# Two attention layers on one core: the values matmuls ahead of the key and query transposes in one half of the loop

## The chip, the cores and the metric

The kernel runs on one core of one Trainium2 chip. The metric is the device time of one execution in microseconds (us), as the median of several executions. The core has a matmul engine (TensorE, PE in the profile), a vector engine (VectorE, DVE), a scalar engine (ScalarE, ACT), a general engine (GpSimd, POOL) and a queue that issues transfers (SyncE, SP). Each engine runs its own list of instructions in order, and the engines wait for each other on semaphores.

## The reference

The input x is 64 sequences of 128 tokens with 512 features. Two layers are applied to it one after the other, and each adds its result to x. A layer is causal attention with 16 query heads of 64 and a single key and value head, with one extra "null" key and value ahead of the 128:

```python
# layer 0                                  # layer 1
xn = layernorm(x, g_in)                    xn = ln(x, g_norm)
q = heads(xn @ Wq) * scale                 q = l2norm(heads(xn @ Wq)) * q_scale
k, v = split(xn @ Wkv)                     k = l2norm(split(xn @ Wkv)[0]) * k_scale;  v = ...
sim = q @ concat(null_k, k).T              sim = 8 * q @ concat(null_k, k).T
sim = mask(sim + bias)                     sim = mask(sim + relative_position_bias)
out = softmax(sim) @ concat(null_v, v)     (the same)
x = x + layernorm(out @ Wo, g_out)         x = x + ln(out @ Wout, g_out)
```

Layer 1 of a sequence needs layer 0 of the same sequence. The sequences are independent of each other.

## The kernel before

All the weights, split into a high and a low part, stay in SBUF. What the engines work on is a unit: one sequence in one layer. Each engine has a `body(a, a_prev, a_next, b_old, b_new)`, in which units of layer 0 are named a and units of layer 1 are named b, and it lists by hand in which order that engine's stages come. One body has two halves. In the first half the engines do the attention of `b_old` while they project and transpose unit `a`. In the second half they do the attention of `a` while they project and transpose `b_new`. `run_stages` leaves out the stages of units that are None. Bodies with both an `a` and a `b_new` number 63: sequences 1 to 63 of layer 0, each with the layer-1 unit of the sequence before it. One further body has a `b_new` and no `a`.

The matmul engine's stages, with the lines that the profile names:

- `transpose_x` (L287) transposes the normalised input, 4 transposes; `project` (L300) computes queries, keys and values, 36 matmuls into the three PSUM banks `Q[0]`, `Q[1]`, `Q[2]`.
- `transpose_k` (L308) is one transpose. It waits for the vector engine (`k_ready`, `q_ready[2]`).
- `transpose_q` (L317) is 8 transposes in two halves of 4. The first half waits for `q_ready[0]` and `q_ready[1]`, the second for `q_ready[2]` and `q_ready[1]`. They signal `qt_done[0]` and `qt_done[1]`.
- `scores` (L330), for groups of heads 0 to 3, multiplies the transposed queries by the keys. Groups 0 and 1 wait for `keys_ready` and `qt_copied[0]`, groups 2 and 3 for `qt_copied[1]`.
- `transpose_p` (L339) transposes the softmax weights, 3 transposes for a group.
- `values` (L354) multiplies them by the values, first for block 1 (`v_diff`), then for block 0 (`v_pair`). Block 1 waits until the scalar engine has copied the transposed weights of all four groups (`pt_copied[0]` to `pt_copied[3]`). The blocks signal `values_done[1]` and `values_done[0]`.
- `project_out` (L368) is three passes of 8 matmuls. Pass 0 waits for `o_hi_done`.

The scalar engine's stages around the change are `inverse_root` (L432, L434: two small operations for the norms of the queries of layer 1, which wait for the vector engine's `norm_floored`), `take_pt` (L455: copies the transposed weights of a group out of PSUM, `pt_copied`), `take_qt` (L440: two copies of the transposed queries, `qt_copied[0]` and `qt_copied[1]`), `rstd_of_output` (L396, L398: waits for `mv_out_done`) and `split_o` (L460: waits for `values_done[1]`, then for `values_done[0]`).

The vector engine ends the second half with `norms(1)` (L515, L519), `normalise` of the next input (L490), `unit_q(1)` (L529, signals `q_ready[1]`), `start_finish` of `b_old` (L569, L571, L577), `take_kt` (L538: the keys out of PSUM, `keys_ready`) and `end_finish` of `b_old` (L585). Then comes the next opening, with `add_bias` (L546) on the first scores. GpSimd adds the mask to the bias of the next unit (`mask_bias`, L622) after it has divided the weights (`divide`, L633).

The order at the end of a half is the function `closing`:

```python
def closing(u, w):
    run_stages((transpose_k, w), (transpose_q, w), (values, u))
```

Of the kernel before, what the change touches and what calls it, by code (L numbers as in the profile page):

```python
# [79 lines left out]
def run_stages(*stages):  # L80
    for stage, u in stages:
        if u:
            stage(u)
# [6 lines left out]
def part(stage, *args):  # L90
    return lambda u: stage(u, *args)
# [18 lines left out]
def build(nc, x, bias0, null_kv, keep0, keep1, L0, L1, out):  # L110
# [16 lines left out]
    with ctx:  # L127
# [154 lines left out]
        def _(pe):  # L282
# [90 lines left out]
            def opening(u, v, w):  # L373
                run_stages((part(scores, (0, 1)), u), (part(project_out, 0), v), (transpose_x, w),
                           (part(project_out, 1), v), (part(scores, (2, 3)), u))

            def closing(u, w):
                run_stages((transpose_k, w), (transpose_q, w), (values, u))

            def body(a, a_prev, a_next, b_old, b_new):  # L380
                opening(b_old, a_prev, a)
                run_stages((part(project_out, 2), a_prev), (part(project, (2,)), a), (part(transpose_p, (0, 1)), b_old),
                           (part(project, (0, 1)), a), (part(transpose_p, (2, 3)), b_old))
                closing(b_old, a)
                opening(a, b_old, b_new)
                run_stages((part(project, (2, 0, 1)), b_new), (part(transpose_p, (0, 1)), a),
                           (part(project_out, 2), b_old), (part(transpose_p, (2, 3)), a))
                closing(a, b_new)

            run_units(pe, body, NB)  # L390

        @program.scalar
        def _(act):
# [69 lines left out]
            def body(a, a_prev, a_next, b_old, b_new):  # L463
                run_stages((part(exponential, (0,)), b_old), (split_x, a), (part(exponential, (1, 2)), b_old),
                           (rstd_of_output, a_prev), (part(exponential, (3,)), b_old),
                           (part(take_pt, (0, 1)), b_old), (part(take_q, 0), a), (rstd_of_input, b_new), (part(take_q, 1), a),
                           (part(take_pt, (2, 3)), b_old), (take_qt, a), (split_o, b_old))
                run_stages((part(exponential, (0,)), a), (split_x, b_new), (part(exponential, (1, 2)), a),
                           (part(square, 2), b_new), (part(exponential, (3,)), a), (part(inverse_root, 2), b_new),
                           (part(square, 0), b_new), (part(inverse_root, 0), b_new), (part(square, 1), b_new),  # L470
                           (rstd_of_input, a_next), (part(take_pt, (0, 1)), a), (part(inverse_root, 1), b_new),
                           (part(take_pt, (2, 3)), a), (take_qt, b_new), (rstd_of_output, b_old), (split_o, a))

            run_units(act, body, NB)

        @program.vector
# [547 lines left out]
```

How the kernel before makes its waits and increments, by code:

```python
def wait(eng, sem, value):  # L44
    if isinstance(value, int) and value <= 0:
        return
    eng.wait_ge(sem, value)
# [2 lines left out]
def wait_apart(eng, sem, value, passed):  # L50
    if not isinstance(value, int):
        eng.wait_ge(sem, value)
        eng.sem_inc(passed, 1)
    else:
        wait(eng, sem, value)
# [184 lines left out]
        @program.sync  # L241
# [25 lines left out]
                    copy_v(b_new)  # L267
                if b_old:
                    wait_apart(sp, layer_done[1], b_old.sdone, sp_passed)
                    sp.dma_start(out[b_old.batch], x_out[:, :]).then_inc(out_stored, 16)
                if b_new:
                    sp.dma_start(x1_res[:, :], x1[:, :]).then_inc(x1_copied, 16)
                    if not (isinstance(b_new.batch, int) and b_new.batch == NB - 1):
                        wait_apart(sp, pad_neg_done, b_new.done, sp_passed)
                        load_keep(1, b_new.batch + 1)
            sp.wait_ge(v_pair_zeroed, 2)
            run_units(sp, body, NB)
            sp.wait_ge(out_stored, 16 * NB)
# [196 lines left out]
        @program.vector  # L476
# [122 lines left out]
                           (part(unit_q, 0), b_new), (part(norms, 1), b_new), (normalise, a_next), (part(unit_q, 1), b_new),  # L599
                           (start_finish, b_old), (take_kt, b_new), (end_finish, b_old))
            for n in range(2):
                nc.vector.memset(v_pair[n][:, :, :], 0.0).then_inc(v_pair_zeroed, 1)
            dve.wait_ge(v_pair_zeroed, 2)
            run_units(dve, body, NB)
```

## Time and profile before

| | |
|---|---|
| median of 3 executions | 2713.48 us (2711.86 to 2715.43) |
| the profiled execution: its own time | 2714.91 us |
| its span, first to last instruction | 2713.1 us |
| PE busy | 2523.7 us (93%) |
| DVE busy | 1849.5 us (68%) |
| ACT busy | 1696.9 us (63%) |
| POOL busy | 1023.0 us (38%) |

The span is what the engines' instructions cover. About 1.8 us of the execution's time lie outside it. A busy share says how long an engine had work in it, not that the work was on the path that sets the end.

### The profile page before, as it was taken

What the parts mean: (1) busy time and instruction counts of PE and PEld (TensorE: products, weight loads), DVE (VectorE), ACT (ScalarE), POOL (GpSimd) and SP (SyncE); (2) the same over time, 40 slices, a digit from 0 to 9 for tenths busy, and PEclk for the clock granted to TensorE, in tenths of its full rate; (3) what the DMA queues carried; (4) which work ended last, traced back from release to release, by engine and by line L of the source; (5) the groups of instructions that cost most, each with busy time, mean ns of one, the idle gap of its engine ahead of it and who ended that gap; (6) DMA issues with size and microseconds to landing.
All of it is one profiled execution on the core that took longest, in us unless ns stands there. A gap on an engine that the chain in (4) does not pass through costs nothing.

```text
span 2713.1 us, 47936 instructions
## 1 busy us (share of the span) xinstructions
PE 2523.7 (93%) x13985; PEld 2093.7 (77%) x13985; DVE 1849.5 (68%) x4665; ACT 1696.9 (63%) x6621; POOL 1023.0 (38%) x1688
## 2 busy tenths in 40 slices
PE   2699999999999999999999999999999999999997
PEld 1577877877878888888788788787787787787884
DVE  5467677667667667667667667767767766766764
ACT  2366666666666666666666666666666666666663
POOL 1343343333433433433433334334334333343331
PEclk7799999999999999999999999999999999999998
DMA  6000010010010010000011011001001001001000
GB/s 204 17 30 28 22 33 29 21 33 29 21 33 29 21 33 29 21 33 29 21 33 33 21 29 33 25 25 33 29 21 33 29 21 33 29 21 33 29 17 20
DMA packets 79317, 85.10 MB, mean 31 GB/s; under 512 B 38944, under 2 KB 42048, under 8 KB 79296
## 3 DMA queue, kind: packets, MB, share of 16 engines
q1 hardware_dynamic: 74864, 82.72, 10.0%
q10 hardware_dynamic: 4432, 2.14, 0.4%
q8 instruction: 9, 0.15, 0.0%
q14 instruction: 12, 0.10, 0.0%
HBM read 49.15 MB, written 16.79 MB: 24 GB/s over the span
## 4 chain that ended last, share of the span: by engine, by line
PE 70%; DVE 14%; ACT 10%; issue 3%; DVEq 0%; POOL 0%
PE psum L368 22%; PE psum L300 15%; PE psum L330 13%; PE psum L354 9%; ACT probs L449 7%; PE psum L317 5%; PE psum L339 3%; DVE q_sb L529 3%; DVE xn L490 2%; DVE norm_sq L515 2%; PE psum L287 2%; DVE bn_in L483 2%; DVE probs L546 1%; DVE neg_max L552 1%; DVE k_dup L527 1%
## 5 line engine op out<-in xcount | busy, mean ns | idle before, releaser
L633 POOL TENSOR_TENSOR weights<-probs,den_inv 128x256 f32<-128x256 f32 (+1 forms) x1024 | 492.6, 507 | 1598.8 <-DVE den_inv L558 1598.8
L449 ACT ACTIVATE probs<-probs,neg_max 128x129 f32<-128x129 f32 (+1 forms) x2048 | 744.1, 366 | 507.4 <-DVE neg_max L552 507.4
L622 POOL TENSOR_TENSOR masked_bias<-bias,pad_neg 128x516 f32<-128x516 f32 (+1 forms) x512 | 477.8, 965 | 15.3 <-POOL pad_neg L616 9.2
L546 DVE TENSOR_TENSOR probs<-psum,masked_bias 128x388 f32<-128x388 f32 x512 | 287.3, 562 | 266.7 <-PE psum L330 247.1
L330 PEld LDWEIGHTS psum<-keys,q_t 128*128 128x128 f32 x2048 | 297.4, 188 | 130.7 <-issue 101.9
L330 PE MATMUL psum<-keys,q_t 128*128 128x130 f32 (+1 forms) x2048 | 392.3, 333 | 2.0 <-DVE keys L538 1.1
L449 ACT ACTIVATION_READ_ACCUMULATOR probs<-probs,neg_max 128x1 f32 x2048 | 387.1, 189 | 0.0
L300 PE MATMUL psum<-w_hi,x_hi 128*128 128x384 f32 x1536 | 348.2, 349 | 3.6 <-DVE x_lo L495 3.6
L300 PE MATMUL psum<-w_hi,x_lo 128*128 128x384 f32 x1536 | 329.7, 337 | 0.0
L300 PE MATMUL psum<-w_lo,x_hi 128*128 128x384 f32 x1536 | 329.5, 337 | 0.0
L368 PE MATMUL psum<-wo_hi,o_hi 128*128 128x512 f32 x1024 | 287.5, 423 | 2.3 <-ACT o_hi L460 2.3
L552 DVE TENSOR_REDUCE neg_max<-probs 128x2 f32<-128x130 f32 (+1 forms) x1024 | 289.5, 345 | 0.0
L300 PEld LDWEIGHTS psum<-w_hi,x_hi 128*128 128x128 f32 x1536 | 271.8, 189 | 13.8 <-DVE x_lo L495 4.4
L368 PE MATMUL psum<-wo_hi,o_lo 128*128 128x512 f32 x1024 | 276.4, 412 | 0.0
L300 PEld LDWEIGHTS psum<-w_lo,x_hi 128*128 128x128 f32 x1536 | 272.9, 188 | 0.0
L300 PEld LDWEIGHTS psum<-w_hi,x_lo 128*128 128x128 f32 x1536 | 272.5, 188 | 0.0
L368 PE MATMUL psum<-wo_lo,o_hi 128*128 128x512 f32 x1024 | 270.3, 406 | 0.0
L339 PE MATMUL psum<-ident,weights 128*128 128x128 f32 x1536 | 214.8, 275 | 20.3 <-ACT probs_t L455 10.7
L368 PEld LDWEIGHTS psum<-wo_hi,o_hi 128*128 128x128 f32 x1024 | 194.9, 191 | 49.8 <-ACT o_hi L460 7.4
L317 PE MATMUL psum<-ident,q_sb 128*128 128x128 f32 x1024 | 137.1, 277 | 91.6 <-DVE q_sb L529 90.5
L455 ACT COPY probs_t<-psum 128x384 f32<-128x384 f32 x512 | 216.6, 475 | 2.3 <-PE psum L339 2.2
L368 PEld LDWEIGHTS psum<-wo_hi,o_lo 128*128 128x128 f32 x1024 | 187.8, 188 | 37.9
(108 smaller groups left out, 3306.7 us busy)
## 6 DMA issues: line engine op xcount, KB each, us to landing
xa<-in_x_dram SPq DMA_DIRECT2D x64, 256.0 KB, 2.9
x_res<-in_x_dram SPq DMA_DIRECT2D x64, 256.0 KB, 2.6
x_res<-x SPq DMA_DIRECT2D x64, 256.0 KB, 2.3
out_dram<-x_out SPq DMA_DIRECT2D x64, 256.0 KB, 2.1
raw<-in_L_cond_Wq_dram SPq DMA_DIRECT2D x8, 512.0 KB, 7.6
raw<-in_L_cond_Wo_dram SPq DMA_DIRECT2D x8, 256.0 KB, 3.4
raw<-in_L_cond_Wout_dram SPq DMA_DIRECT2D x8, 256.0 KB, 3.7
v_pair<-v_diff SPq DMA_DIRECT2D x128, 16.0 KB, 1.7
```

The source lines that it names most:

```text
L300: m = nc.tensor.matmul(Q[b][:, 0:hi - lo], xs[:, c * P:(c + 1) * P], ws[u.layer][:, c, lo:hi], start=(n == 0), stop=(n == 3 * KC - 1))
L317: tr = nc.tensor.transpose(rows[:, j // 2, :, j % 2, :], q_sb[:, q:q + P], ident[:, :])
L330: m = nc.tensor.matmul(block(SP[g % 2], b), q_t[:, g, b, :], keys[u.layer][:, :, 0:WIDTH[b]], start=True, stop=True)
L339: t = nc.tensor.transpose(SP[g % 2][:, k * P:(k + 1) * P], weights[:, g, k, :], ident[:, :])
L354: m = nc.tensor.matmul(O[b][e * DH:(e + 1) * DH, :], v, probs_t[:, :, e if b == 1 else 2, :], start=True, stop=True)
L368: m = nc.tensor.matmul(Y[:, 0:D], os[:, j * P:(j + 1) * P], ws[u.layer][:, j, :], start=(p == 0 and j == 0), stop=(p == 2 and j == PAIRS - 1))
L449: x_ = nc.scalar.activation(s, s, ACT.Exp, bias=neg_max[:, g, b, e:e + 1], accum_out=den[:, g, b, e:e + 1])
L455: nc.scalar.copy(probs_t[:, g, :, :], SP[g % 2][:, 0:3 * P].rearrange("p (k i) -> p k i", k=3)).then_inc(pt_copied[g], 1)
L546: nc.vector.tensor_tensor(probs[:, g, :], SP[g % 2][:, 0:ROW], masked_bias[u.layer][:, g, :], ALU.add).then_inc(biased[g], 1)
L552: m = nc.vector.tensor_reduce(neg_max[:, g, b, :], block(probs[:, g, :], b), AX.X, ALU.max, negate=True)
L622: m = nc.gpsimd.tensor_tensor(block(masked_bias[u.layer][:, gs, :], b), block(bias[u.layer][:, gs, :], b), pad_neg[u.layer][:, 0:WIDTH[b]] ...
L633: m = nc.gpsimd.tensor_tensor(w, block(probs[:, g, :], b)[:, :, 1:1 + n], den_inv[:, g, b, :].unsqueeze(2).to_broadcast([P, 2, n]), ALU.mult)
```

## The change

In the second half of the body the matmul engine's stages are reordered. `values` of `a` comes directly after the last `transpose_p`, and `transpose_k` and `transpose_q` of `b_new` follow it. The first half keeps `closing(b_old, a)`, which has the transposes first. On the scalar engine the second half's tail is reordered as well: `take_qt` of `b_new` moves from ahead of `rstd_of_output` and `split_o` to behind them. Nothing is added or removed.

```diff
                 opening(a, b_old, b_new)
                 run_stages((part(project, (2, 0, 1)), b_new), (part(transpose_p, (0, 1)), a),
-                           (part(project_out, 2), b_old), (part(transpose_p, (2, 3)), a))
-                closing(a, b_new)
+                           (part(project_out, 2), b_old), (part(transpose_p, (2, 3)), a),
+                           (values, a), (transpose_k, b_new), (transpose_q, b_new))
...
                            (rstd_of_input, a_next), (part(take_pt, (0, 1)), a), (part(inverse_root, 1), b_new),
-                           (part(take_pt, (2, 3)), a), (take_qt, b_new), (rstd_of_output, b_old), (split_o, a))
+                           (part(take_pt, (2, 3)), a), (rstd_of_output, b_old), (split_o, a), (take_qt, b_new))
```

## Rows read from the trace of the kernel before

**Rows 1.** Who waited for whom, whole execution: waiter, releaser, us in total, times, longest.
```profile
PE psum L317 <- DVE q_sb L529: 90.5, 64, 1.5
```
**Rows 2.** Windows: length, busy us of PE, PEld, DVE, ACT, POOL, granted clock, DMA share, GB/s.
```profile
1200.00:1242.00 42.00, 40.52 (x230) 33.91 (x229) 29.18 (x76) 27.07 (x109) 16.97 (x29) 1.00 0.08 27
```
**Rows 3.** Timeline of PE, end of a second half: start, us, instructions, idle before and releaser.
```profile
1229.77 0.86 PE L339 MATMUL psum<-ident,weights 128*128 128x128 f32 x6
1230.47 0.27 PE L308 MATMUL psum<-ident,k_dup 128*128 128x128 f32 x1
1232.22 1.06 PE L317 MATMUL psum<-ident,q_sb 128*128 128x128 f32 x8 [1.48 <-DVE q_sb L529]
1233.21 1.08 PE L354 MATMUL psum<-probs_t,v_diff 128*64 128x512 f32 x4
...
1235.08 1.58 PE L330 MATMUL psum<-keys,q_t 128*128 128x130 f32 x8
```
**Rows 4.** Timeline of ACT in the same stretch.
```profile
1230.69 0.21 ACT L432 ACTIVATE norm_ln<-norm_sq 128x6 f32<-128x6 f32 x1 [0.72 <-DVE norm_sq L519]
...
1231.13 0.84 ACT L455 COPY probs_t<-psum 128x384 f32<-128x384 f32 x2
1232.88 1.07 ACT L440 COPY q_t<-psum 128x512 f32<-128x512 f32 x2 [0.91 <-PE psum L317]
1233.84 0.31 ACT L396 ACTIVATE ln_out<-mv_out,eps_col 128x1 f32<-128x1 f32 x1
1234.18 0.20 ACT L398 ACTIVATE rstd_out<-ln_out 128x1 f32<-128x1 f32 x1
1234.34 0.69 ACT L460 ACTIVATE o_hi<-psum,null_v_col 128x512 fp32r<-128x512 f32 x1
1235.19 0.69 ACT L460 ACTIVATE o_hi<-psum,null_v_col 128x512 fp32r<-128x512 f32 x1 [0.17 <-PE psum L354]
1237.82 0.40 ACT L449 ACTIVATE probs<-probs,neg_max 128x129 f32<-128x129 f32 x1 [1.94 <-DVE neg_max L552]
```
**Rows 5.** Timeline of DVE in the same stretch.
```profile
1229.59 1.07 DVE L519 TENSOR_SCALAR norm_sq<-norm_sq 128x6 f32<-128x6 f32 x1
...
1231.53 0.55 DVE L529 TENSOR_TENSOR q_sb<-psum,norm_inv 128x384 f32<-128x384 f32 x1
...
1232.83 0.18 DVE L571 BATCH_NORM_AGGREGATE mv_out<-bn_out 128x2 f32<-128x6 f32 x1 [0.16 <-DVE bn_out L569]
...
1233.82 0.71 DVE L538 TENSOR_SCALAR keys<-psum,k_scale 64x128 f32<-64x128 f32 x2
1234.55 0.75 DVE L585 SCALAR_TENSOR_TENSOR x_out<-x_out,rstd_out,x_res 128x512 f32<-128x512 f32 x1
1236.11 1.15 DVE L546 TENSOR_TENSOR probs<-psum,masked_bias 128x388 f32<-128x388 f32 x2 [0.80 <-PE psum L330]
```
**Rows 6.** Timeline of POOL in the same stretch.
```profile
1228.47 3.73 POOL L622 TENSOR_TENSOR masked_bias<-bias,pad_neg 128x516 f32<-128x516 f32 x4 [0.15 <-POOL pad_neg L616]
```
**Rows 7.** Timeline of PE, ACT and DVE, end of a first half.
```profile
1211.06 0.27 PE L308 MATMUL psum<-ident,k_dup 128*128 128x128 f32 x1
1211.22 1.06 PE L317 MATMUL psum<-ident,q_sb 128*128 128x128 f32 x8
1212.22 1.08 PE L354 MATMUL psum<-probs_t,v_diff 128*64 128x512 f32 x4
...
1213.35 0.69 ACT L460 ACTIVATE o_hi<-psum,null_v_col 128x512 fp32r<-128x512 f32 x1 [0.38 <-PE psum L354]
...
1211.37 0.72 DVE L538 TENSOR_SCALAR keys<-psum,k_scale 64x128 f32<-64x128 f32 x2 [1.19 <-PE psum L308]
```
**Rows 8.** Timeline of PE and ACT, first layer-0 unit, which has no values between.
```profile
90.33 1.06 PE L317 MATMUL psum<-ident,q_sb 128*128 128x128 f32 x8 [0.55 <-ACT q_sb L415]
91.73 1.55 PE L330 MATMUL psum<-keys,q_t 128*128 128x130 f32 x8 [0.33 <-ACT q_t L440]
...
91.00 1.07 ACT L440 COPY q_t<-psum 128x512 f32<-128x512 f32 x2 [0.81 <-PE psum L317]
```
**Rows 9.** One line's instructions, whole execution: count, ns min/median/max.
```profile
L440 ACT COPY q_t<-psum x256: 585/587/593, 91.0 to 2681.8; 128x512 f32<-128x512 f32 x128
...
L519 DVE TENSOR_SCALAR norm_sq<-norm_sq x192: 170/246/1069, 136.0 to 2679.1; 128x6 f32<-128x6 f32 x128, 128x5 f32<-128x5 f32 x64
```

## The prediction

> **What bounds the kernel now.** I began with the list of waits. The matmul engine has one wait worth money in the loop: the query transposes (L317) wait for the vector engine's L529, 90.5 us in all, 64 times, 1.5 us at the longest, so it is nearly the same in every pass [rows 1]. A window of a whole pass then shows PE busy for 40.52 of 42 us at a granted clock of 1.00, the full 2.4 GHz [rows 2]. So PE is the bound, except in that one gap of about 1.4 us per pass, where it hangs on a chain of DVE and ACT. The timelines of PE, ACT and DVE around the gap [rows 3 to 5] show what is in it. PE issues its last weight transposes at 1229.77 and the key transpose at 1230.47, stands still for 1.48 us, transposes queries at 1232.22, starts `values` at 1233.21 and the next scores at 1235.08 [rows 3]. From there to the next such gap I found no wait of PE. Whatever the change does to the start of the scores is therefore carried through the whole following pass, and the start of the scores is the quantity to compute.
>
> **What `values` would wait for.** The change puts `values` into the gap. But block 1 of `values` needs `pt_copied[3]`, the second of two copies that ACT makes from 1231.13 for 0.84 us, so until 1231.97 [rows 4]. PE was finished with those transposes long before. The copies are late because ACT works in order and `inverse_root(1)` stands ahead of them: its L432 sat idle for 0.72 us on L519 of DVE [rows 4], and that L519 took 1.07 us [rows 5]. The change leaves this order alone. From the end of a releaser to PE's first instruction I take 0.14 us: L529 ends at 1231.53 + 0.55 = 1232.08 [rows 5] and PE starts at 1232.22 [rows 3]. In the first unit it is the same: the copy ends at 91.00 + 0.59 = 91.59 and PE starts at 91.73 [rows 8, 9]. So `values` starts at 1231.97 + 0.14 = 1232.11. The query transposes now start at 1232.22. The gap is not filled; it ends 0.11 us earlier.
>
> **PE after that.** `values` takes 1235.08 - 1233.21 = 1.87 us [rows 3]. The key transpose follows at 1233.98. Today it costs nothing, since it lies ahead of the gap; now it is on the path, and from it to the first query transpose is 1211.22 - 1211.06 = 0.16 us [rows 7]. The query transposes start at 1234.14. They keep PE for 1.00 us [rows 7], so if nothing else is waited for the scores start at 1235.14, which is 0.06 us later than the 1235.08 of today [rows 3]. That is the lower bound for a pass in which `values` starts where I say.
>
> **The wait that comes in its place.** Today `values` lies between the query transposes and the scores, and its 1.87 us cover the copy of the transposed queries (L440) and of the keys (L538). In the new order nothing lies between, and the scores of group 0 wait for `qt_copied[0]`. The first unit of the kernel has exactly this order, with ACT idle: transposes at 90.33, copy at 91.00, scores at 91.73 [rows 8]. So from the first query transpose to the scores is 1.40 us where it could be 1.00, and the scores start at 1234.14 + 1.40 = 1235.54. I take 0.02 off, because two readings of the step from keys to queries differ by that much (the busy time of one transpose against the next start), and use 1235.52. That is 0.44 us later than today.
>
> **Is ACT free for that copy?** It has to start at 1234.14 + (91.00 - 90.33) = 1234.81 [rows 8]. Ahead of it the change puts `rstd_of_output` and `split_o`. `mv_out` is there at 1232.83 + 0.18 = 1233.01 [rows 5], so L396 can run at about 1233.05. L396 to L398 takes 0.34 us and L398 to the next instruction 0.16 us (1233.84, 1234.18, 1234.34 [rows 4]), which makes 1233.55. The first `split_o` can start 1213.35 - 1212.22 = 1.13 us after `values` [rows 7], at 1233.24, so it starts at 1233.55. The second can start 1235.19 - 1233.21 = 1.98 us after `values` [rows 3, 4], at 1234.09, but the first one, 0.69 us long, lets it go at about 1234.15 (successive ACT instructions start some 0.1 us before the end of the one ahead: 1.07 us for two copies of 0.587 [rows 4, 9]). ACT is then free at about 1234.75, which is 0.06 us before the copy's data are there. ACT order adds nothing, but with no margin. If those instructions didn't overlap at all, from 1233.55 through two `split_o` of 0.69 and a copy of 0.59 with a hop of 0.14 the scores would start at 1235.66, 0.58 later than today. That is the upper bound for this term.
>
> **The keys.** The key transpose at 1233.98 gives DVE its L538 1211.37 - 1211.06 = 0.31 us later [rows 7], at 1234.29, for 0.71 us. That makes the keys ready at 1235.00 and releases PE at 1235.14, well inside the wait for the queries. DVE is free then, since today L538 starts at 1233.82 right behind `start_finish` [rows 5]. Behind L538 stands `end_finish` (L585, 0.75 us), which would end at about 1235.7. The next instruction of DVE, `add_bias`, starts 1236.11 - 1235.08 = 1.03 us after the scores [rows 3, 5], at 1236.55, so it isn't delayed. SP's store of the output waits for `end_finish`, and it shifts along with the pass. ACT's next work, the exponentials at 1237.82 [rows 4], comes 2.7 us after the scores, while the second query copy ends some 0.5 us after the first. What is gained is that `split_o` is finished earlier, before the scores, but `project_out` never waited for it in the loop, so this is worth nothing. No transfer is issued by a moved stage, and none is moved past.
>
> **The sum.** Per pass: -0.11 (the gap ends earlier) and +0.16 (the key transpose on the path), with the hundredth that rounding leaves +0.06; then +0.38 (the scores wait for the copy); together +0.44 us, with bounds of +0.06 and +0.58. There are 63 passes with both units. In the one pass without an `a` there is no `values` to move, and I count it as nothing. DVE and ACT being close together, some passes may do a little better, so I take 0.42: 63 x 0.42 = 26.5 us. The profiled execution would go from 2714.91 to 2741.4 us, its span from 2713.1 to 2739.6. Its own time is 1.4 us above the median of 2713.48, so I forecast a median of 2740 us, 1.0% slower. A measurement of this kernel tells 0.2%, 5.4 us or 0.09 us per pass, from no change.
>
> **A rule that bears on the start of the gap.** L519 takes 0.17 us at its shortest and 1.07 us at its longest [rows 9], and the long one lies while GpSimd's L622 runs, from 1228.47 to 1232.20 [rows 5, 6]. The Trainium skill (SBUF — State Buffer, section "Who interferes with whom") says that a vector `tensor_scalar` in a two-port mode and a GpSimd instruction exclude each other for a whole instruction, whoever comes first. By that rule L519 is held until one of the four L622 ends, and its cost depends on where it falls against them. The row agrees in size with one such instruction, and this is the third rival below; the sum above goes by the row.
>
> **Rivals.**
> *The gap is filled.* `values` would run in the 1.48 us, and the scores would follow 1.40 us after 1232.22, at 1233.62: 1.46 us earlier per pass, 92 us in all, about 2621 us. For it speaks only that PE idles there [rows 3]. Against it stand the copies that end at 1231.97 [rows 4], in an order which the change doesn't touch. Chance 0.03.
>
> *The copy stays hidden*, the two effects cancel and the scores start at 1235.14: +0.06 per pass, about 2717 us. Against it speaks the same sequence in the first unit, with its wait [rows 8]. Chance 0.05.
>
> *L519 falls clear of GpSimd.* L519 would take 0.25 instead of 1.07 us (the median of all [rows 9]). Its end would come 0.82 earlier, and with it ACT's copies, of which the transposes of 1229.77 allow about 0.66. From 0.44 later this makes about 0.22 us earlier per pass, 14 us, about 2700 us. It decides for faster from 0.53 us of earlier copies on (0.44 and the 0.09 of the measurement). Against it: both instructions follow from the exponentials upstream of the change, so that their distance should stay. Chance 0.06.
>
> *A second late party.* If `start_finish` on DVE or the `split_o` waits on ACT come late by another 0.3 to 0.5 us, the copy or the keys start later and the loss is 0.75 to 0.95 us per pass, 2761 to 2773 us. The margin of ACT is only 0.06 us, and of the keys 0.4 us. Chance 0.06.
>
> **Numbers.** The forecast has 0.80. The range reaches from 2722 (+0.13 per pass) to 2751 us (+0.6 per pass), which holds nearly all of the forecast's own cases. Faster by over 0.2%: the first and third rival, 0.09. Within 0.2%: the second and the lowest forecasts, 0.06. Slower: 0.85.
>
> **What would show it.** In the profile after, the wait of L317 for L529 is gone. PE's `values` waits for ACT's L455 instead, for about 1.2 to 1.4 us, 63 times. The scores (L330) wait for ACT's L440 for about 0.35 us, 63 times. A pass takes about 0.4 us more. L519 keeps its maximum of 1.07. I am wrong if `values` starts well before the old start of the query transposes (L455 not the last releaser), if the scores wait for nothing, or if L330 waits for L538 and not for L440.

## The result and the profile after

The changed kernel takes 2754.63 us in the median of four executions (2753.02 to 2755.19), the kernel before 2713.74 (2711.86 to 2715.43). The ratio is 1.0150 with a 95% interval of 1.0132 to 1.0167: 41 us slower. I had forecast 2740 us and a range up to 2751. The sign was right, and so was the mechanism in its outline, but the loss is one and a half times what I had worked out, and outside the range.

The list of waits of the changed kernel, with the rows that answer to [rows 1] (waiter, releaser, us in total, times, longest):

```profile
PE psum L354 <- ACT probs_t L455: 100.6, 66, 1.6
...
PE psum L330 <- ACT q_t L440: 25.8, 61, 0.4
```

The wait of L317 for L529, 90.5 us before [rows 1], is gone from the list. In its place stands a longer one, of `values` for the copies of the transposed weights, and a second one, of the scores for the copy of the queries. The same window as in [rows 2] shows PE with less work done in 42 us at the same granted clock of 1.00, so the clock has no part in the loss:

```profile
1200.00:1242.00 42.00, 39.95 (x226) 33.52 (x224) 28.67 (x74) 27.14 (x109) 15.68 (x26) 1.00 0.08 27
```

The timeline of PE at the end of a second half of the changed kernel, with the start of `values` one pass later (answers to [rows 3]):

```profile
1207.30 0.87 PE L339 MATMUL psum<-ident,weights 128*128 128x128 f32 x6
1209.79 1.08 PE L354 MATMUL psum<-probs_t,v_diff 128*64 128x512 f32 x4 [1.63 <-ACT probs_t L455]
...
1211.66 0.33 PE L308 MATMUL psum<-ident,k_dup 128*128 128x128 f32 x1
1211.83 1.04 PE L317 MATMUL psum<-ident,q_sb 128*128 128x128 f32 x8
1213.29 1.58 PE L330 MATMUL psum<-keys,q_t 128*128 128x130 f32 x8 [0.42 <-ACT q_t L440]
...
1250.79 1.08 PE L354 MATMUL psum<-probs_t,v_diff 128*64 128x512 f32 x4 [1.58 <-ACT probs_t L455]
```

And of ACT in that stretch (answers to [rows 4]):

```profile
1208.21 0.21 ACT L432 ACTIVATE norm_ln<-norm_sq 128x6 f32<-128x6 f32 x1 [0.71 <-DVE norm_sq L519]
...
1208.66 0.84 ACT L455 COPY probs_t<-psum 128x384 f32<-128x384 f32 x2
1210.57 0.29 ACT L396 ACTIVATE ln_out<-mv_out,eps_col 128x1 f32<-128x1 f32 x1 [1.08 <-DVE mv_out L571]
1210.90 0.20 ACT L398 ACTIVATE rstd_out<-ln_out 128x1 f32<-128x1 f32 x1
1211.01 1.45 ACT L460 ACTIVATE o_hi<-psum,null_v_col 128x512 fp32r<-128x512 f32 x2
1212.46 1.07 ACT L440 COPY q_t<-psum 128x512 f32<-128x512 f32 x2
```

A pass takes 1250.79 - 1209.79 = 41.00 us. Before it took 40.36, from the query transposes of two neighbouring passes (1232.22 less 1191.86, a row like the third of [rows 3]). The difference of 0.64 us times 63 passes is 40.3 us, and the spans differ by 2753.4 - 2713.1 = 40.3 us. So the loss lies in the passes, but that the two agree to a tenth of a us is luck. Of the 63 passes 60 are run by the loop, and they lose 0.65 us each: over 34 of them the mean is (2604.29 - 1209.79) / 34 = 41.01 us against (2604.47 - 1232.22) / 34 = 40.36 before. That is 39 us. The other three, whose code stands outside the loop, lose 2.2, 0.5 and 1.0 us, and two stretches outside the passes give back 0.5 us (the first scores, 91.20 against 91.73) and 2.0 us (the last unit, from 2688.64 to 2723.09 against 2646.34 to 2682.77).

Set against the last weight transposes (L339), the scores started 5.31 us later before [rows 3] and start 1213.29 - 1207.30 = 5.99 us later now. In the next pass it is 5.94. My steps had given 5.75: 2.34 to the start of `values`, 1.87 for it, 0.16 for the key transpose, 1.38 from the query transposes to the scores. Measured are 2.49, 1.87, 0.17 and 1.46.

The two large misses are each the step from the end of a copy on ACT to PE's next instruction. The second L455 ends at 1208.66 + 0.84 = 1209.50 and PE starts at 1209.79: 0.29 us. The first L440 ends at 1212.46 + 0.59 = 1213.05 and PE starts at 1213.29: 0.24 us. I had taken 0.14 for both. The pass shown is one of the longer ones: the first step is 0.30 us in 19 of 58 passes counted in the loop and 0.25 in the other 39, which is what lies between 5.99 and 5.94, and the second is 0.24 in all 58. Why a third of the passes has the longer first step isn't known.

### The profile page after: what moved, and what is told of

It is laid out like the page before. It is cut to its first block, busy times and chain, and to the rows that moved or that the text cites. A ratio compares the mean times of both kernels' runs of the same rounds, so it can differ in the third digit from the quotient of the medians.

```text
span 2753.4 us, 47936 instructions
## 1 busy us (share of the span) xinstructions
PE 2528.9 (92%) x13985; PEld 2097.8 (76%) x13985; DVE 1855.0 (67%) x4665; ACT 1699.5 (62%) x6621; POOL 1022.0 (37%) x1688
## 4 chain that ended last, share of the span: by engine, by line
PE 67%; ACT 15%; DVE 12%; issue 2%; DVEq 0%; POOL 0%
PE psum L368 22%; PE psum L300 15%; PE psum L330 13%; PE psum L354 9%; ACT probs L449 7%; PE psum L339 3%; DVE norm_sq L519 2%; PE psum L317 2%; DVE norm_sq L515 2%; PE psum L287 2%; ACT probs_t L455 2%; DVE q_sb L529 2%; ACT o_hi L460 2%; DVE bn_in L483 2%; DVE probs L546 1%
## 5 line engine op out<-in xcount | busy, mean ns | idle before, releaser
L622 POOL TENSOR_TENSOR masked_bias<-bias,pad_neg 128x516 f32<-128x516 f32 (+1 forms) x512 | 477.7, 964 | 15.3 <-POOL pad_neg L616 9.2
L354 PE MATMUL psum<-probs_t,v_diff 128*64 128x512 f32 x512 | 141.7, 629 | 100.6 <-ACT probs_t L455 100.6
L339 PE MATMUL psum<-ident,weights 128*128 128x128 f32 x1536 | 215.7, 276 | 20.0 <-ACT probs_t L455 10.7
L455 ACT COPY probs_t<-psum 128x384 f32<-128x384 f32 x512 | 216.7, 474 | 2.9 <-PE psum L339 2.8
```

Source lines behind the costliest of these rows:

```text
L339: t = nc.tensor.transpose(SP[g % 2][:, k * P:(k + 1) * P], weights[:, g, k, :], ident[:, :])
L354: m = nc.tensor.matmul(O[b][e * DH:(e + 1) * DH, :], v, probs_t[:, :, e if b == 1 else 2, :], start=True, stop=True)
L455: nc.scalar.copy(probs_t[:, g, :, :], SP[g % 2][:, 0:3 * P].rearrange("p (k i) -> p k i", k=3)).then_inc(pt_copied[g], 1)
L622: m = nc.gpsimd.tensor_tensor(block(masked_bias[u.layer][:, gs, :], b), block(bias[u.layer][:, gs, :], b), pad_neg[u.layer][:, 0:WIDTH[b]] ...
```

## The experiments

The kernels were timed in turn with the kernel before on the same chip. Ratios are to that, and the median of before moved between 2710.4 and 2714.6 us from one group of runs to the next, each on a chip of its own. So a difference in us between kernels of different groups, the changed kernel included, is uncertain by some 4 us. A pass read from the traces is the finer measure.

**The scalar engine's half alone.** The matmul engine keeps the old order.

```diff
-  (part(take_pt, (2, 3)), a), (take_qt, b_new), (rstd_of_output, b_old), (split_o, a))
+  (part(take_pt, (2, 3)), a), (rstd_of_output, b_old), (split_o, a), (take_qt, b_new))
```

> The scalar engine's half of the change alone: take_qt behind split_o, with the matmul engine's old order. Theory (the scores wait for the copy of the queries): the copy now starts after the second split_o, 1.98 + 0.6 us after values, and ends 3.2 us after values instead of before them, so the scores start some 1.4 us later than before in each of 63 passes, +85 to +95 us, about 2800 us. Rival (the scalar engine's order doesn't matter, only the matmul engine's does): within 5 us of 2714.

Measured: 2807.57 us, ratio 1.0341 (1.0324 to 1.0359), 93 us slower. PE's timeline in this kernel:

```profile
1233.10 1.06 PE L317 MATMUL psum<-ident,q_sb 128*128 128x128 f32 x8 [1.48 <-DVE q_sb L529]
...
1237.48 1.58 PE L330 MATMUL psum<-keys,q_t 128*128 128x130 f32 x8 [1.45 <-ACT q_t L440]
```

The old gap is still there, and the scores wait 1.45 us for the copy, which now stands behind both `split_o`. The theory holds, with 93 us where it had 85 to 95. This half only makes sense beside the other.

**The matmul engine's half alone.** `take_qt` stays ahead of `rstd_of_output` and `split_o`.

```diff
-  (part(project_out, 2), b_old), (part(transpose_p, (2, 3)), a))
-  closing(a, b_new)
+  (part(project_out, 2), b_old), (part(transpose_p, (2, 3)), a),
+  (values, a), (transpose_k, b_new), (transpose_q, b_new))
```

> The matmul engine's half alone: values ahead of the transposes, with take_qt still ahead of rstd_of_output and split_o. Theory (the copy of the queries starts when its transposes are there, in either order of the scalar engine): as the changed kernel, 2750 to 2756 us, with the scores waiting 0.4 us for L440. Rival (the scalar engine, busy with split_o, makes the copy late): the first copy starts up to 0.1 us earlier and the time falls by about 6 us, to 2748.

Measured: 2794.3 us, ratio 1.0296 (1.0279 to 1.0313). Both expectations missed by 40 us. PE's timeline in this kernel shows why:

```profile
1228.01 1.04 PE L317 MATMUL psum<-ident,q_sb 128*128 128x128 f32 x8
1229.47 1.58 PE L330 MATMUL psum<-keys,q_t 128*128 128x130 f32 x8 [0.42 <-ACT q_t L440]
1231.43 1.90 PE L368 MATMUL psum<-wo_hi,o_hi 128*128 128x512 f32 x7 [0.38 <-ACT o_hi L460]
```

On the scores I was right: the step from the query transposes is 1.46 us, exactly as in the changed kernel, so `split_o` on ACT doesn't delay that copy. What I hadn't looked at is the instruction behind: `project_out` now waits for `split_o`. It starts 1.96 us after the scores where it was 1.22 in the changed kernel (1214.51 against 1213.29). The pass grows by a little less than that, from 41.01 to 41.63 us (1267.61 less 1225.98, two starts of `values` in this kernel), and 0.62 us times 63 is 39. The prediction said that the earlier `split_o` was worth nothing. That was true against the kernel before, but given the new order of PE it is what the scalar engine's half is there for, worth 40 us.

**The wait for `o_lo_done` ahead of those for the copies.** Everything else is as in the changed kernel.

```diff
                 for b in (1, 0):
+                    wait(pe, o_lo_done[b], u.prev)
                     if b == 1:
                         wait(pe, v_ready, u.done)
                         for g in range(NG):
                             wait(pe, pt_copied[g], u.done)
...
-                    wait(pe, o_lo_done[b], u.prev)
```

> The changed kernel with one wait of values moved: the one for o_lo_done, long met, stands ahead of those for v_ready and pt_copied and no longer behind the one that is met last. Theory A (each wait instruction behind the late one costs its own time after the release): values start 0.10 to 0.15 us after the copy's end and no longer 0.25 to 0.29, -0.12 us per pass, -7 to -9 us, about 2746 us. Rival B (the longer step comes from the matmul engine's long idleness or from the kind of matmul): no change, 2754 +- 2 us, step 0.25 to 0.29.

**The wait for the previous unit's `pt_copied` ahead of those for the keys and the queries.** Also on the changed kernel.

```diff
                 for g in groups:
+                    if g < 2:
+                        wait(pe, pt_copied[g + 2], u.prev)
                     if g == 0:
                         wait(pe, keys_ready, u.done)
                     wait(pe, qt_copied[g // 2], u.done)
-                    if g < 2:
-                        wait(pe, pt_copied[g + 2], u.prev)
-                    else:
+                    if g >= 2:
                         wait(pe, biased[g - 2], u.done)
```

> The changed kernel with one wait of the first scores moved: the one for the previous unit's pt_copied stands ahead of those for keys_ready and qt_copied. Theory A (a wait behind the late one costs time): from the end of the first L440 to the scores 0.14 us and no longer 0.24, -0.10 us per pass, -6 us, about 2748 us. Rival B: no change, 2754 +- 2 us.

Measured: 2745.77 us for the first (ratio 1.0112, 1.0095 to 1.0129), 9 us less than the changed kernel, and 2748.85 us for the second (1.0124, 1.0107 to 1.0141), 6 us less. The intervals are as wide as the effects, so the traces decide. In them a pass of the loop takes 40.89 us in the first and 40.87 in the second, 0.12 and 0.14 us less than the changed kernel's 41.01. ACT and PE of the first kernel, the copy and the start of `values`:

```profile
1206.20 0.84 ACT L455 COPY probs_t<-psum 128x384 f32<-128x384 f32 x2
...
1207.19 1.08 PE L354 MATMUL psum<-probs_t,v_diff 128*64 128x512 f32 x4 [1.48 <-ACT probs_t L455]
```

Of the second, the copy and the start of the scores:

```profile
1210.35 1.07 ACT L440 COPY q_t<-psum 128x512 f32<-128x512 f32 x2
...
1211.08 1.55 PE L330 MATMUL psum<-keys,q_t 128*128 128x130 f32 x8 [0.33 <-ACT q_t L440]
```

The copy of the first ends at 1207.04 and PE starts 0.15 us later, not 0.29. The copy of the second ends at 1210.94 and PE starts 0.14 us later, not 0.24. Both are theory A, and each step is the same in all the passes of the loop.

One thing limits it. In three places the code of these scores stands outside the loop, and there they don't pay for the wait behind. Right behind the loop, PE and ACT:

```profile
2647.32 1.04 PE L317 MATMUL psum<-ident,q_sb 128*128 128x128 f32 x8
2648.64 1.55 PE L330 MATMUL psum<-keys,q_t 128*128 128x130 f32 x8 [0.29 <-issue]
...
2647.95 1.07 ACT L440 COPY q_t<-psum 128x512 f32<-128x512 f32 x2
```

The copy ends at 2648.54 and PE starts 0.10 us later, with the same list of waits. The step to `values` stays at 0.25 us outside the loop. The trace's records of PE's waits, which the views above leave out, point to the reason. In the loop two wait records stand between the end of the copy and the weight load of the scores, the second of them on a register operation; outside the loop none stands there. In the second kernel, with the wait moved, one is left. A wait that is carried by the weight load itself isn't a further record. So what was paid for is a separate instruction behind the late wait, and a line `wait(...)` isn't always one. That is read from records; no run changed the register operation alone.

**Two more waits behind the late one.** They are for a semaphore that is met already.

```diff
                     wait(pe, o_lo_done[b], u.prev)
+                    if b == 1:
+                        wait(pe, o_lo_done[b], u.prev)
+                        wait(pe, o_lo_done[b], u.prev)
```

> The changed kernel with the wait for o_lo_done written three times instead of once behind the late wait of values; the two added ones are met at once. Theory A (each wait instruction behind the late one costs 0.11 to 0.14 us): the step from the copy to values grows from 0.28 to about 0.53 us, +0.24 us per pass, +15 us, about 2770 us. Rival (the move of e3 gained for another reason, and waits that are met cost nothing): 2754.

Measured: 2775.44 us, ratio 1.0241 (1.0226 to 1.0257), 21 us above the changed kernel where I expected 15. ACT and PE of this kernel (its lines stand 3 further down):

```profile
1216.43 0.84 ACT L458 COPY probs_t<-psum 128x384 f32<-128x384 f32 x2
...
1217.79 1.08 PE L357 MATMUL psum<-probs_t,v_diff 128*64 128x512 f32 x4 [1.86 <-ACT probs_t L458]
```

The step grew from 0.29 to 1217.79 - 1217.27 = 0.52 us, 0.115 for each wait, as expected. In most passes it is 0.47 where it was 0.25, 0.11 for each. The rest is in the first half, where PE waits for nothing. From the query transposes to the scores it takes 1240.72 - 1237.77 = 2.95 us there, against 2.87 in [rows 7] (1214.09, the scores that follow there, less 1211.22). The rows of this kernel:

```profile
1237.77 1.06 PE L317 MATMUL psum<-ident,q_sb 128*128 128x128 f32 x8
...
1240.72 1.58 PE L330 MATMUL psum<-keys,q_t 128*128 128x130 f32 x8
```

So 0.23 us in the second half and 0.08 to 0.09 in the first, 0.32 us a pass, which times 63 is 20.2. The spans differ by 2773.6 - 2753.4 = 20.2 us. That they agree so closely is in part luck, as the kernels ran on different chips (by their ratios they lie 25 us apart), but the passes of the loop differ by 0.32 us too, 41.33 against 41.01.

**The same two waits moved in the kernel before.**

> The kernel before with the two waits moved as in e3 and e4. Theory (a wait costs only where it stands behind the one that is met last, and in the old order both are met while the matmul engine is still at work): no change, 2712 +- 3 us. Rival (each semaphore wait costs time anywhere, or the order changes something else): 5 us or more faster.

Measured: 2710.65 us, ratio 0.9998 (0.9989 to 1.0007). No change, as the theory has it. There the late wait of the query transposes (`q_ready[1]`) already was the last of its stage, and the stages with a wait behind it didn't stand still. The waits are moved here and none is added, so this run doesn't say what one costs in such a stretch.

**The key transpose ahead of `values`.** On the changed kernel.

```diff
-  (values, a), (transpose_k, b_new), (transpose_q, b_new))
+  (transpose_k, b_new), (values, a), (transpose_q, b_new))
```

> The changed kernel with transpose_k ahead of values, in the idle time. Theory (the key transpose costs 0.16 us on the path there): -0.16 us per pass, -10 us, about 2744 us. Rival (the scores wait for take_qt anyway, which is held by split_o, so nothing is gained): 2754.

Measured: 2747.17 us, ratio 1.0125 (1.0108 to 1.0142), 7.5 us less than the changed kernel. The key transpose did cost time on the path, as the theory has it. Of its 0.16 us per pass, 10 us in all, two thirds to three quarters come back: in this kernel's timeline the scores start 1.52 us after the query transposes (1208.86 less 1207.34) and not 1.46. The copy of the queries starts 0.70 us after them where it was 0.63 (1208.04, right behind `split_o`), so here ACT's order does hold it a little.

**The copies ahead of `inverse_root(1)`.** On the changed kernel, scalar engine.

```diff
-  (part(take_pt, (0, 1)), a), (part(inverse_root, 1), b_new),
-  (part(take_pt, (2, 3)), a), (rstd_of_output, b_old), (split_o, a), (take_qt, b_new))
+  (part(take_pt, (0, 1, 2, 3)), a), (part(inverse_root, 1), b_new),
+  (rstd_of_output, b_old), (split_o, a), (take_qt, b_new))
```

> The changed kernel with the scalar engine's take_pt(2, 3) ahead of inverse_root(1), so that the copies for values no longer wait for L519. Counting from the start of the last weight transposes, values should start at about 1.75 us and no longer 2.45. Theory (two chains hang on L519, the copies and, through L529 and start_finish, mv_out, for which rstd_of_output and behind it split_o and take_qt wait): with values early, take_qt is held by the second chain instead, the scores stay at 5.9 us and the time near 2753 us (2745 to 2758). Rival (only the copies hold the end of the pass): the scores move 0.7 us earlier, -44 us, about 2710.

Measured: 2745.18 us, ratio 1.0119 (1.0102 to 1.0136). PE and ACT of this kernel:

```profile
1202.58 0.86 PE L339 MATMUL psum<-ident,weights 128*128 128x128 f32 x6
1204.22 1.08 PE L354 MATMUL psum<-probs_t,v_diff 128*64 128x512 f32 x4 [0.77 <-ACT probs_t L455]
...
1208.37 1.58 PE L330 MATMUL psum<-keys,q_t 128*128 128x130 f32 x8 [1.08 <-ACT q_t L440]
...
1205.98 0.29 ACT L396 ACTIVATE ln_out<-mv_out,eps_col 128x1 f32<-128x1 f32 x1 [1.57 <-DVE mv_out L571]
```

`values` starts 1.64 us after the last weight transposes, 0.8 us earlier, and the wait ahead of it is 0.77 us and no longer 1.6. Little comes of it: some 9 us, at the lower end of what the theory allowed. ACT stands 1.57 us on the statistics of the output, with `split_o` and `take_qt` behind it, and the scores start at 5.79 us. So a second chain runs beside the first, and ends only a little earlier.

**Without the floor of the middle group (L519).** Once on the changed kernel, once on the kernel before. The maximum with the floor is left out for those six heads, so neither computes quite the same. The arguments of the reduction are left out below.

```diff
-  nc.vector.tensor_reduce(...).then_inc(norm_summed[b], 1)
+  r = nc.vector.tensor_reduce(...)
+  if b == 1:
+      r.then_inc(norm_floored[b], 1)
+      return
+  r.then_inc(norm_summed[b], 1)
```

> The changed kernel without the floor under the squared norms of the middle group of heads (L519 for group 1; the reduction signals in its place), which leaves that maximum out of the computation. Theory (L519, 1.05 us long beside GpSimd's L622, holds both chains): copies and mv_out both come 0.6 to 0.7 us earlier, the scores too, -40 us, about 2714 us. Rival (the next vector instruction, L490, takes over the whole stall, or the copies are then held by the transposes): less than half of that, above 2734.

> The kernel before without the floor of the middle group's squared norms (that maximum is left out of the computation). Theory (the same L519 holds the old order's query transposes, through L490 and L529): 0.65 to 0.8 us earlier per pass, -40 to -50 us, about 2667 us, so that the changed order stays 40 us behind it with or without L519. Rival (L519 held only the copies): less than 20 us.

Measured: 2706.76 us on the changed kernel (ratio 0.9978, 0.9968 to 0.9989), 48 us less than with it; 2669.56 us on the kernel before (0.9848, 0.9833 to 0.9864), 41 us less. One small instruction of 1.07 us, which runs beside GpSimd's L622, stands on the path of both orders, as the root of both chains. The two kernels without it lie 37 us apart (35 by their ratios), nearly as far as with it. So the loss of the change doesn't come from L519; it comes from what follows.

**Five moves together.** On the changed kernel: both late waits last, the key transpose ahead of `values`, the copies ahead of `inverse_root(1)`, and these two orders:

```diff
 # scalar engine
-  (rstd_of_output, b_old), (split_o, a), (take_qt, b_new))
+  (split_o, a), (part(take_qt, (0,)), b_new), (rstd_of_output, b_old), (part(take_qt, (1,)), b_new))
 # vector engine
-  (start_finish, b_old), (take_kt, b_new), (end_finish, b_old))
+  (take_kt, b_new), (start_finish, b_old), (end_finish, b_old))
```

> The changed kernel with five moves together: both late waits last (as in e3 and e4), transpose_k ahead of values, take_pt(2, 3) ahead of inverse_root(1), on the scalar engine split_o, the first query copy, rstd_of_output, the second query copy, and on the vector engine take_kt ahead of start_finish. Theory: values at 1.6 us after the last weight transposes, query transposes at 3.5, scores at about 4.9 to 5.0 where the kernel before has 5.31: -0.35 us per pass, about 2692 us, faster than before. Rival (the late statistics of the output now delay end_finish and through it the softmax of the next pass): above 2714.

Measured: 2684.32 us, ratio 0.9892 (0.9875 to 0.9908). PE of this kernel:

```profile
1217.93 0.86 PE L339 MATMUL psum<-ident,weights 128*128 128x128 f32 x6
1218.62 0.27 PE L308 MATMUL psum<-ident,k_dup 128*128 128x128 f32 x1
1219.46 1.08 PE L354 MATMUL psum<-probs_t,v_diff 128*64 128x512 f32 x4 [0.56 <-ACT probs_t L455]
...
1221.33 1.09 PE L317 MATMUL psum<-ident,q_sb 128*128 128x128 f32 x8
1222.75 1.55 PE L330 MATMUL psum<-keys,q_t 128*128 128x130 f32 x8 [0.33 <-ACT q_t L440]
```

The scores start 4.82 us after the last weight transposes, 0.49 us earlier than in the kernel before, and the time is 8 us below the 2692 that I expected. The two new orders weren't tried by themselves, so how much each of the five moves brings in this kernel stays open.

**The input transposes in the last wait.** On top of the five moves, in the first half's opening:

```diff
-  opening(b_old, a_prev, a)
+  run_stages((transpose_x, a), (part(scores, (0, 1)), b_old), (part(project_out, 0), a_prev),
+             (part(project_out, 1), a_prev), (part(scores, (2, 3)), b_old))
```

> The kernel of the five moves, and in the first half's opening the four input transposes (L287) ahead of the first scores instead of behind project_out's first pass, so that they lie in the wait for the copy of the queries (0.33 us there). Theory: the scores start 0.1 us later, but 0.44 us of input transposes go from later in the pass: -0.3 us per pass, -15 to -22 us, about 2665 us. Rival (the softmax chain of the unit, which begins with those scores, becomes the bound): no gain, 2680 to 2690 us.

Measured: 2656.0 us, ratio 0.9795 (0.9781 to 0.9808), the fastest kernel of the study. PE of this kernel:

```profile
1207.87 1.09 PE L317 MATMUL psum<-ident,q_sb 128*128 128x128 f32 x8
1208.80 0.60 PE L287 MATMUL psum<-ident,xn 128*128 128x128 f32 x4
1209.30 1.55 PE L330 MATMUL psum<-keys,q_t 128*128 128x130 f32 x8
```

The scores start 1.43 us after the query transposes, no later than they did with the wait (1.42), and wait for nothing. The four transposes are done inside it. A pass of the loop is 0.43 us shorter (39.85 to 39.42), which is the whole 0.44 us that I had put down for them, and the gain is 28 us where I expected 15 to 22.

## Why the prediction was wrong, point by point

**What bounds the kernel, and where the change acts.** Right. PE carries the pass from the scores on, and the later start of the scores, 0.65 us in each of the 60 passes of the loop, is 39 of the 40 us.

**What `values` waits for.** Right. The second L455 starts 1.36 us after the last weight transposes, before (1231.13 less 1229.77 [rows 3, 4]) and after (1208.66 less 1207.30), and its 0.84 us end at the 2.20 that I used. L519 is as long as before, and its 1.07 us stand at the root of it, as the run without it showed.

**The step of 0.14 us from a releaser to PE.** This is the step that failed, a term of the sum that was sized too small: "From the end of a releaser to PE's first instruction I take 0.14 us". Measured are 0.29 to `values` and 0.24 to the scores. Both rows from which I took it [rows 3, 8, 9] are of stages in which the kernel's text has no wait behind the one that is met last. The query transposes wait for `q_ready[1]` last. In the first unit the wait for the previous unit is left out by `wait()`, since its value is zero. In the loop, `values` has the wait for `o_lo_done` behind that for `pt_copied[3]`, and the scores have that for `pt_copied` of the previous unit behind that for `qt_copied[0]`. The runs with these waits moved brought the step back to 0.15 and 0.14 us, and two added waits lengthened it by 0.22 to 0.23 us. So it is shown, not argued, for the passes of the loop; the scores outside it have the same list of waits and a step of 0.10 us. These two, 0.15 and 0.10 us, are 0.25 us in the pass of the rows, and 0.21 in the two thirds of the passes in which `values` starts 0.25 us after the copy. The copy of the queries was ready some 0.04 us sooner than I had it, the 0.02 that I had taken off was not there, and the key transpose took 0.01 more. Together that is the 0.24 between 5.75 and 5.99.

**The 0.02 per pass taken off in the sum**, because "some passes may do a little better". They didn't. A pass of the loop loses 0.65 us in the mean, 0.68 in the pass of the rows and 0.63 in the next, so 0.44 should have stood as it was.

**The wait that takes the place of the old cover.** Right, and sized right but for the step above: from the query transposes to the scores it takes 1.46 us where I had 1.38. In the list of waits it is 0.42 us, 61 times, where I had said about 0.35. The wait of `values` for L455 is 1.58 to 1.63 us, where I had said 1.2 to 1.4. The run of PE's half alone shows that ACT's order adds nothing to it in the changed kernel.

**What is gained is worth nothing.** Right as a term of the sum, wrong as a reading. The earlier `split_o` pays for a wait of `project_out` that PE's new order would bring with it.

**The range.** Its upper end took only ACT's overlap as unknown, and the step of 0.14 us went into the sum at `values` and at the scores with no bound of its own. With the measured 0.29 and 0.24 in its place the upper bound would have been 0.58 + 0.25 = 0.83 us per pass, and the range would have held the time.

**The rivals.** The second late party, at 0.75 to 0.95 us per pass, came nearest in size but not in kind: neither `start_finish` nor `split_o` was late. In place of a filled gap, `values` started 0.04 us later than the query transposes did before, counted from the last weight transposes (2.49 against 2.45).

## What to carry to other kernels

An engine's wait is filled only by work whose own inputs are there. Before work is moved into a gap, look up when its releaser ends, and what it covered where it stood. Here the `values` matmuls had been hiding two copies, and without them the scores waited for one.

Where an engine stands still on one of several semaphores, put the wait that is met last at the end of the list; a separate wait instruction behind it is paid after the release, and the trace says whether one stands there. And when a chain is cut, look for the one that ends next: making the copies for `values` earlier brought 9 us, where 0.7 us per pass would have been 44, because the statistics of the output held ACT next.

## What the runs showed of the hardware

A semaphore wait of the matmul engine that is met already isn't free. Behind a late wait at `values` it took about 0.11 us (0.14 with none, 0.25 with one, 0.47 with three, each in most passes of the loop). In a stretch where PE had work all the time it took about 0.04 us (2.87 to 2.95 for two). From the end of an ACT copy to PE's first matmul the step was 0.14 us with no wait behind, and 0.10 at the scores outside the loop, the shortest.

The long L519 stayed at 1.07 us in the changed kernel, and when the instruction was taken out, part of the stall moved on. Without it the next `tensor_scalar`, L490, took 1.44 us in place of 1.03, as the timeline of DVE in the changed kernel without the floor shows:

```profile
1228.69 1.44 DVE L490 TENSOR_SCALAR xn<-xa,mv_in,rstd_in 128x512 f32<-128x512 f32 x1
1230.06 0.55 DVE L533 TENSOR_TENSOR q_sb<-psum,norm_inv 128x384 f32<-128x384 f32 x1
```

That agrees with the rule of exclusion of the Trainium skill that the prediction cites (SBUF — State Buffer, section "Who interferes with whom"), if L490 now waits for one of the L622. The rule itself doesn't say that a stall moves on; that is read from this row. That L519 is held by L622 and by nothing else wasn't tried by moving L622, so this stays open.
